# Two matmuls of 256 columns made into one of 512 in three of the seven products of a Strassen-like pair

## The chip, the cores and the metric

The kernel runs on one core of a Trainium2 chip. The metric is the device time of one execution in microseconds (us), as the median of several runs. Before the change it is 586.91 us (three runs, 586.62 to 586.93).

## The reference, cut to what matters

A mixture of eight experts with two tasks, for a batch of 512 rows:

```python
h = relu(einsum('bi,eio->beo', x, eW1) + eb1)           # 1024 -> 1024, per expert
h = relu(einsum('beh,eho->beo', h, eW2) + eb2)          # 1024 -> 512
expert_out = einsum('beh,eho->beo', h, eW3) + eb3       # 512 -> 256
gates = softmax(einsum('bi,tie->bte', x, gW) + gb, axis=-1)
tin = einsum('bte,bed->btd', gates, expert_out)
th = relu(einsum('btd,tdh->bth', tin, tW1) + tb1)       # 256 -> 512
th = relu(einsum('bth,tho->bto', th, tW2) + tb2)        # 512 -> 256
out = sigmoid(einsum('bth,tho->bto', th, tW3) + tb3)[..., 0]
```

All of it is float32.

## The kernel before

**Precision.** TensorE multiplies in the format fp32r. Each operand is split into a high part (the value rounded to fp32r) and a low part (the rest). One product is then three matmuls into one PSUM bank: high weights by high data, high weights by low data, low weights by high data (`triple`, L263 to L266). ScalarE makes the high parts (names ending in `_hi`), VectorE the low ones by a subtraction (names ending in `_lo`).

**Stages.** Layer 1 of expert 0 is done plainly, in 512-column matmuls, then layer 2 of expert 0. A loop follows with e from 1 to 7. In it TensorE does layer 1 of expert e as four *pairs*, then layer 3 of the expert before (24 matmuls of 512 columns), then layer 2 of expert e (96 matmuls of 512 columns). Behind the loop stand the last layer 3 and the two towers.

**A pair.** Layer 1 of experts 1 to 7 uses the seven products of a Strassen-Winograd scheme instead of eight. The 1024 outputs, the 1024 inputs and the batch are each cut in two; a pair i makes the output blocks i and 4 + i of 128 rows for both halves of the batch (256 columns each). `PRODUCTS` (L53) lists for each of the seven: the bank and the half of it that it writes, whether it reads x or `t` (differences of blocks of x, formed once), and which block. Each product has four contraction blocks of three matmuls with 256 columns, thus 84 matmuls a pair. A pair uses the banks 0 to 3 or, when i is odd, 4 to 7. In their order the products are called P2, P1, P4, P7, P5, P6, P3.

**Preparing a pair.** VectorE forms four sums of weight blocks (`sum31`, `sum2`, `sum4`; L763, L769, L775), ScalarE casts the three plain blocks and the four sums (`plain_hi`, `sums31_hi`, `sums24_hi`; L571, L577, L585 to L589), and VectorE makes the low parts (`plain_lo`, `sums31_lo`, `sums24_lo`, all through `split_lo`, L727). The weights lie in a ring of ten slots.

**Combining a pair.** ScalarE takes P1 out of its bank (`p1_take`, L597 and L598). VectorE adds the products up into `quarter`: `combine_base` (L808: P2 and P6 plus or minus P1), `combine_united` (L813: plus P7 and P5), `combine_lower` (L819), `combine_cross` (L825 and L828: P3 and P4). Its last operation raises the semaphore `combined`. ScalarE then writes the ReLU's high part (`pair_h1`, L602) and VectorE the low one (`pair_h1_lo`, through L738).

**What sets the order.** Each engine runs its own list, written by hand, and semaphores tie the lists. VectorE's list in the loop has three iterations (i = 0 to 2) that prepare pair i + 1 and, from i = 1, combine pair i - 1. Behind them stand a tail that combines pair 2, the splits of W3 and of three pieces of W2 (`w3_lo`, `w2_lo`), a tail that combines pair 3, the last piece of W2 and the gating of the expert before (`gate_expert`). TensorE waits for `slot_ready` (weights split) at the first, fourth and sixth product of a pair; for `combined` of pair i - 2 at the first product of pair i; and for `combined` of pair 3 at the start of layer 2, whose four banks (`BANK_HIDDEN2`) pair 3 has used. SP issues the weight loads, each held by a wait for `slot_ready`.

```python
                for i in range(PAIRS - 1):
                    if i > 0:
                        combine_base(e, i - 1)
                    sum31(e, i + 1)
                    if i > 0:
                        combine_united(e, i - 1)
                    sum2(e, i + 1)
                    if i > 0:
                        combine_lower(e, i - 1)
                        combine_cross(e, i - 1)
                    sum4(e, i + 1)
                    plain_lo(e, i + 1)
```

Of the kernel before, what the change touches and what calls it, by code (L numbers as in the profile page):

```python
# [13 lines left out]
P = 128  # L14
# [11 lines left out]
MG = 4  # L26
# [26 lines left out]
PRODUCTS = [(1, 0, "x", 1, 0),  # L53
            (0, 0, "x", 0, 0),
            (3, 0, "t", 1, 0),
            (2, 1, "t", 0, 1),
            (2, 0, "t", 0, 0),
            (1, 1, "t", 1, 1),
            (3, 1, "x", 1, 1)]
# [14 lines left out]
BANK_HIDDEN1 = [0, 1, 2, 3, 4, 5, 6, 7]  # L74
BANK_HIDDEN2 = [4, 5, 6, 7]
BANK_OUT3 = [0, 1]
BANK_LOGITS, BANK_GATES = 0, 1
BANK_TOWER1 = [[2, 3, 4, 5], [6, 7, 0, 1]]
BANK_TOWER2 = [[2, 3], [4, 5]]
BANK_FINAL = [6, 7]  # L80
# [35 lines left out]
def moe_towers(nc, xT, eW1_first, eW1_pairs, eW2, eW3, tW1, tW2, small, out):  # L116
    with ExitStack() as ctx:
# [6 lines left out]
        x_hi, x_lo = sb("x_hi", [KX, BATCH], F32R), sb("x_lo", [KX, BATCH], F32R)  # L124
        t_hi, t_lo = sb("t_hi", [KX, BATCH], F32R), sb("t_lo", [KX, BATCH], F32R)
        h1_hi, h1_lo = sb("h1_hi", [K2, BATCH], F32R), sb("h1_lo", [K2, BATCH], F32R)
# [13 lines left out]
        banks = [ctx.enter_context(nc.psum_tensor(f"bank{b}", [P, BATCH], F32)) for b in range(8)]  # L140
# [35 lines left out]
        def pair_of(h, i):  # L176
            return h[:].rearrange("p (g i) b -> p g i b", g=2)[:, :, i, :]
# [23 lines left out]
        lowered = sem("lowered")  # L201
        combined = sem("combined")
# [128 lines left out]
        def _(pe):  # L331
# [33 lines left out]
            def pair(e, i):  # L365
                ready = splits(e) + 3 * i
                for n, (bank, nh, source, kh, xh) in enumerate(PRODUCTS):
                    if n == 0:
                        if i == 0:

                            pe.wait_ge(gated_ready, 1 + GATED * (e - 1))
                        elif i == 1:
                            pe.wait_ge(h2_staged, K3 * e)
                        else:
                            pe.wait_ge(combined, PAIRS * (e - 1) + i - 1)
                        pe.wait_ge(slot_ready, ready + 1)
                    if n == 3:
                        pe.wait_ge(slot_ready, ready + 2)
                    if n == 5:
                        pe.wait_ge(slot_ready, ready + 3)  # L380
                    slot = (NP * i + n) % RING
                    to = banks[4 * (i % 2) + bank][:, nh * HALF:(nh + 1) * HALF]
                    hi, lo = (x_hi, x_lo) if source == "x" else (t_hi, t_lo)
                    for kk in range(KK):
                        cols = slice(kk * P, (kk + 1) * P)
                        mm = triple(pe, to, w_hi[:, slot, cols], w_lo[:, slot, cols],
                                    block_of(hi, kh, xh)[:, kk, :], block_of(lo, kh, xh)[:, kk, :],
                                    kk == 0, kk == KK - 1)
                    mm.then_inc(slot_used, 1)

            def layer2(e, between=None):
                first = isinstance(e, int)
                order = by_tile(range(0, 6), MG) + by_bank(range(6, 8), MG)
                for i, (n, m) in enumerate(order):
                    k = ORDER2[n]
                    if m == 0:
                        if n % 2 == 0:
                            pe.wait_ge(slot_ready, (KX + n // 2 + 1) if first
                                       else splits(e) + 3 * PAIRS + 1 + n // 2 + 1)
                        if first:  # L400
# [9 lines left out]
                    mm = triple(pe, banks[BANK_HIDDEN2[m]][:], w_hi[:, n, cols], w_lo[:, n, cols],  # L410
                                h1_hi[:, k, :], h1_lo[:, k, :], n == 0, n == K2 - 1)
# [86 lines left out]
            for t in range(T):  # L498
                pe.wait_ge(slot_ready, ready + T + t + 1)
                for i, (k, m) in enumerate(by_bank(range(KT2), KT1)):  # L500
                    if i < KT2:
                        pe.wait_ge(tower1_ready, t * KT2 + k + 1)
                    if k == 0:
                        pe.wait_ge(tower1_staged, 2 * t + m + 1)
                    slot = 2 * T + 2 * t + k // 2
                    cols = slice((k % 2) * TH2 + m * P, (k % 2) * TH2 + (m + 1) * P)
                    mm = triple(pe, banks[BANK_TOWER2[t][m]][:], w_hi[:, slot, cols], w_lo[:, slot, cols],
                                h1_hi[:, t * KT2 + k, :], h1_lo[:, t * KT2 + k, :], k == 0, k == KT2 - 1)
                    if k == KT2 - 1:
                        mm.then_inc(tower2_done, 1)  # L510
# [9 lines left out]
        def _(act):  # L520
# [21 lines left out]
            def take_first(m):  # L542
                act.wait_ge(sums_done, m + 1)
                bank, bias = banks[BANK_HIDDEN1[m]], prm_of("b1", m)
                act.activation(h1_hi[:, m, :], bank[:], ACT.Relu, bias=bias).then_inc(h1_taken, 1)
# [45 lines left out]
            def p1_take(e, i):  # L591
# [4 lines left out]
                p = banks[4 * (i % 2)][:, 0:HALF]  # L596
# [3 lines left out]
            def pair_h1(e, i):  # L600
                act.wait_ge(combined, PAIRS * (e - 1) + i + 1)
                act.activation(pair_of(h1_hi, i), stage[:], ACT.Relu).then_inc(h1_taken, 1)  # L602
# [50 lines left out]
            with act.Fori(1, E) as e:  # L653
# [67 lines left out]
        def _(dve):  # L721
# [18 lines left out]
            def first_h1_lo(m):  # L740
                dve.wait_ge(h1_staged, m + 1)
                relu_lo(h1_lo[:, m, :], stage[:, m % 2, :], h1_hi[:, m, :]).then_inc(h1_ready, 1)
# [53 lines left out]
            def bank_of(i, b):  # L796
                return banks[4 * (i % 2) + b][:].rearrange("p (h b) -> p h b", h=2)

            def combine_base(e, i):
# [8 lines left out]
                dve.tensor_tensor(quarter[:, 0:5:4, :], bank_of(i, 1), p1[:], ALU.add).then_inc(based, 1)  # L808

            def combine_united(e, i):  # L810

                dve.wait_ge(based, PAIRS * (e - 1) + i + 1)
                dve.tensor_tensor(quarter[:, 1:3, :], bank_of(i, 2), quarter[:, 4:5, :].broadcast_to([P, 2, HALF]),  # L813
                                  ALU.add).then_inc(united, 1)

            def combine_lower(e, i):

                dve.wait_ge(united, PAIRS * (e - 1) + i + 1)
                dve.scalar_tensor_tensor(quarter[:, 3, :], bank_of(i, 2)[:, 0, :], prm_of("b1", e * K2 + MG + i),  # L819
                                         quarter[:, 2, :], ALU.add, ALU.add).then_inc(lowered, 1)  # L820

            def combine_cross(e, i):

                dve.wait_ge(slot_used, used(e, NP * i + 6))
                dve.scalar_tensor_tensor(quarter[:, 1, :], bank_of(i, 3)[:, 1, :], prm_of("b1", e * K2 + i),  # L825
                                         quarter[:, 1, :], ALU.add, ALU.subtract)
                dve.wait_ge(lowered, PAIRS * (e - 1) + i + 1)
                dve.scalar_tensor_tensor(quarter[:, 2, :], bank_of(i, 3)[:, 0, :], prm_of("b1", e * K2 + MG + i),  # L828
                                         quarter[:, 2, :], ALU.add, ALU.add).then_inc(combined, 1)

            def pair_h1_lo(e, i):
                dve.wait_ge(h1_taken, K2 + PAIRS * (e - 1) + i + 1)
                relu_lo(pair_of(h1_lo, i), stage[:], pair_of(h1_hi, i)).then_inc(h1_ready, 1)
# [107 lines left out]
            with dve.Fori(1, E) as e:  # L941
# [9 lines left out]
                for i in range(PAIRS - 1):  # L951
# [18 lines left out]
                combine_cross(e, PAIRS - 2)  # L970
                pair_h1_lo(e, PAIRS - 2)
# [6 lines left out]
                combine_cross(e, PAIRS - 1)  # L978
                pair_h1_lo(e, PAIRS - 1)
# [130 lines left out]
```

## Time and profile before

| | us |
|---|---|
| median of three runs | 586.91 (586.62 to 586.93) |
| the profiled execution, its own time | 586.58 |
| its span, from first to last instruction | 584.9 |
| TensorE matmul busy | 577.5 (99%) |
| TensorE weight load busy | 520.9 (89%) |
| VectorE busy | 436.1 (75%) |
| ScalarE busy | 263.9 (45%) |
| GpSimd busy | 44.2 (8%) |

The granted clock of TensorE is 1.00 of full speed over the span. Matmuls are pipelined: each is shown for 283 ns (256 columns) or 389 ns (512 columns), while the next one begins earlier. What a matmul costs in a full stream is therefore the distance from start to start, not its duration. On VectorE too an instruction that waits for nothing begins before the one ahead of it has ended.

### The profile page before, as it was taken

How to read it: one execution, taken by the hardware profiler on the slowest of the kernel's cores; microseconds unless marked ns; L12 is line 12 of the kernel's file. 1: busy time of each engine (PE TensorE's matmuls, PEld its weight loads, DVE VectorE, ACT ScalarE, POOL GpSimd, SP SyncE). 2: the span in 40 equal slices, each digit the busy share in tenths (PEclk: the TensorE clock that was granted, in tenths of full speed). 3: DMA queues.
4: the chain of work that ended last, by engine and by line, in shares of the span. 5: the costliest groups of instructions: out<-in, count | busy, mean ns of one | idle time of the engine just before them, and what ended most of it. 6: DMA issues, size and time to landing. Idle time of an engine off the chain costs nothing.

```text
span 584.9 us, 9687 instructions
## 1 busy us (share of the span) xinstructions
PE 577.5 (99%) x3637; PEld 520.9 (89%) x3637; DVE 436.1 (75%) x534; ACT 263.9 (45%) x334; POOL 44.2 (8%) x46
## 2 busy tenths in 40 slices
PE   8999999999999999999999999999999999999997
PEld 5888889988999899988999889998999889998775
DVE  7954199874997569874898649985698749975492
ACT  3545174515645174522653255341645146542552
POOL 0000010030000300021000300003000300004000
PEclk9999999999999999999999999999999999999999
DMA  8340333243141513234223422316032332353000
GB/s 305 138 143 10 135 112 145 74 168 119 72 143 36 198 53 143 72 117 170 72 73 106 179 72 83 132 36 251 4 140 101 143 114 72 119 165 111 1 1 0
DMA packets 23276, 63.27 MB, mean 108 GB/s; under 512 B 1617, under 2 KB 6865, under 8 KB 19682
## 3 DMA queue, kind: packets, MB, share of 16 engines
q1 hardware_dynamic: 21906, 58.64, 28.3%
q0 software_dynamic: 1216, 4.23, 2.1%
q10 hardware_dynamic: 144, 0.26, 0.2%
q8 instruction: 7, 0.11, 0.1%
q14 instruction: 3, 0.02, 0.0%
HBM read 63.08 MB, written 0.04 MB: 108 GB/s over the span
## 4 chain that ended last, share of the span: by engine, by line
PE 95%; DVE 2%; DMA 1%; ACT 1%; issue 1%; SPq 0%; DVEq 0%
PE bank L264 31%; PE bank L266 31%; PE bank L265 31%; DMA w_raw<-eW_first 1%; DVE w_lo L727 1%; PE bank L441 0%; PE bank L442 0%; DVE scratch L763 0%; ACT w_hi L687 0%; ACT w_hi L530 0%; PE bank L516 0%; SPq L284 0%; DVE scratch L1043 0%; DVE scratch L1003 0%; ACT h_hi L624 0%
## 5 line engine op out<-in xcount | busy, mean ns | idle before, releaser
L264 PE MATMUL bank<-h_hi,w_hi 128*128 128x512 f32 x336 | 131.1, 390 | 0.8 <-DVE h_lo L738 0.8
L265 PE MATMUL bank<-h_lo,w_hi 128*128 128x512 f32 x336 | 130.8, 389 | 0.0
L266 PE MATMUL bank<-h_hi,w_lo 128*128 128x512 f32 x336 | 130.7, 389 | 0.0
L727 DVE TENSOR_TENSOR w_lo<-w_raw,w_hi 128x1024 fp32r<-128x1024 f32 (+1 forms) x79 | 111.3, 1420 | 25.5 <-ACT w_hi L540 8.1
L264 PE MATMUL bank<-x_hi,w_hi 128*128 128x256 f32 (+1 forms) x412 | 125.2, 304 | 1.8 <-DVE w_lo L727 1.1
L264 PE MATMUL bank<-t_hi,w_hi 128*128 128x256 f32 x448 | 126.8, 283 | 0.0
L265 PE MATMUL bank<-t_lo,w_hi 128*128 128x256 f32 x448 | 126.8, 283 | 0.0
L266 PE MATMUL bank<-t_hi,w_lo 128*128 128x256 f32 x448 | 126.8, 283 | 0.0
L265 PE MATMUL bank<-x_lo,w_hi 128*128 128x256 f32 (+1 forms) x412 | 124.7, 303 | 0.0
L266 PE MATMUL bank<-x_hi,w_lo 128*128 128x256 f32 (+1 forms) x412 | 124.7, 303 | 0.0
L738 DVE SCALAR_TENSOR_TENSOR h_lo<-scratch,h_hi 128x512 fp32r<-128x512 f32 (+1 forms) x68 | 61.8, 912 | 55.0 <-ACT scratch L625 34.9
L264 PEld LDWEIGHTS bank<-t_hi,w_hi 128*128 128x128 f32 x448 | 86.0, 192 | 0.0
L265 PEld LDWEIGHTS bank<-t_lo,w_hi 128*128 128x128 f32 x448 | 86.0, 192 | 0.0
L266 PEld LDWEIGHTS bank<-t_hi,w_lo 128*128 128x128 f32 x448 | 86.0, 192 | 0.0
L264 PEld LDWEIGHTS bank<-x_hi,w_hi 128*128 128x128 f32 x412 | 78.7, 191 | 6.6 <-DVE w_lo L727 2.1
L571 ACT ACTIVATE w_hi<-w_raw 128x1536 fp32r<-128x1536 f32 x28 | 41.8, 1492 | 93.8 <-PE bank L266 93.8
L265 PEld LDWEIGHTS bank<-x_lo,w_hi 128*128 128x128 f32 x412 | 78.7, 191 | 3.1
L266 PEld LDWEIGHTS bank<-x_hi,w_lo 128*128 128x128 f32 x412 | 78.7, 191 | 3.0
L264 PEld LDWEIGHTS bank<-h_hi,w_hi 128*128 128x128 f32 x336 | 63.1, 188 | 14.1 <-DVE h_lo L738 1.2
L266 PEld LDWEIGHTS bank<-h_hi,w_lo 128*128 128x128 f32 x336 | 63.1, 188 | 13.2
L265 PEld LDWEIGHTS bank<-h_lo,w_hi 128*128 128x128 f32 x336 | 63.1, 188 | 12.8
L727 DVE TENSOR_TENSOR w_lo<-scratch,w_hi 128x1024 fp32r<-128x1024 f32 x49 | 58.8, 1226 | 20.8 <-ACT w_hi L577 19.0
(95 smaller groups left out, 540.2 us busy)
## 6 DMA issues: line engine op xcount, KB each, us to landing
w_raw<-eW_pairs SPq DMA_DIRECT2D x28, 1024.0 KB, 4.8
w_raw<-eW SPq DMA_DIRECT2D x40, 512.0 KB, 3.7
scratch<-gates_dram POOLq DMA_DIRECT2D x8, 512.0 KB, 3.8
w_raw<-eW_first SPq DMA_DIRECT2D x7, 512.0 KB, 6.2
w_raw<-tW SPq DMA_DIRECT2D x4, 512.0 KB, 4.2
scratch<-xT SPq DMA_DIRECT2D x7, 256.0 KB, 6.4
w_raw<-eW_first SPq DMA_DIRECT2D x2, 256.0 KB, 4.2
scratch<-xT ACTq DMA_DIRECT2D x1, 256.0 KB, 3.4
```

What stands on the lines that cost most here:

```text
L264: pe.matmul(bank, weights_hi, moving_hi, start=first, stop=False)
L265: pe.matmul(bank, weights_hi, moving_lo, start=False, stop=False)
L266: return pe.matmul(bank, weights_lo, moving_hi, start=False, stop=last)
L571: act.activation(wide(pair_slots(i, 0, 3)), w_raw[:, u * UNIT:u * UNIT + 3 * SLOT], ACT.Copy) \
L727: dve.tensor_tensor(wide(w_lo, slots), raw, wide(w_hi, slots).bitcast(F32), ALU.subtract).then_inc(slot_ready, 1)
L738: return dve.scalar_tensor_tensor(lo, staged, 0.0, hi.bitcast(F32), ALU.max, ALU.subtract)
```

## The change

1. `PRODUCTS` now has for each product two places among the 16 half banks (for even and for odd i) and a flag. Where the flag is set (P2, P4 and P3) the matmul of the high weights reads the high and the low part of the x block at once, as two strips of 256 columns, and writes a whole bank: high by high into its first half, high by low into its second. The matmul of the low weights still has 256 columns and adds to the first half. The other four products stay as they were.
2. x and t hold their high and low parts in one tile each (`x_both`, `t_both`). The eight banks are one tensor. `h1_hi` and `h1_lo` are laid out by batch halves, so that layer 2 and the second tower layer read their 512 columns as two strips of 256.
3. The banks are given out anew. An even pair has 0, 1 and 2 for itself, an odd one 5, 6 and 7; bank 3 (P7 and P5) and bank 4 (P3) are shared by all pairs. Banks of layer 2: 5, 6, 7, 4.
4. TensorE gets new waits: at the fourth product for `lowered` of the pair before, at the sixth for `p1_staged` of its own pair, at the seventh for `combined` of the pair before (in pair 0 for `h2_staged`).
5. VectorE gets `combine_low`: two more adds a pair, which add the second halves of the three banks (512 and 256 elements). They now raise `combined`. `combine_lower` moves up behind `combine_united`. `combine_cross` waits for `lowered` ahead of both its operations.
6. ScalarE does `p1_take` before `pair_h1`, `sums31_hi` and `sums24_hi` instead of between the last two, and `p1_take` of pair 3 before `pair_h1` of pair 2 and the split of W3.

```diff
-PRODUCTS = [(1, 0, "x", 1, 0),
...
+PRODUCTS = [((0, 10), True, "x", 1, 0),
+            ((4, 14), False, "x", 0, 0),
+            ((2, 12), True, "t", 1, 0),
+            ((6, 6), False, "t", 0, 1),
+            ((7, 7), False, "t", 0, 0),
+            ((5, 15), False, "t", 1, 1),
+            ((8, 8), True, "x", 1, 1)]
+P2, P1, P4, P7, P5, P6, P3 = [places for places, *_ in PRODUCTS]
...
-BANK_HIDDEN2 = [4, 5, 6, 7]
+BANK_HIDDEN2 = [5, 6, 7, 4]
...
+        x_both, t_both = sb("x_both", [2, KX, BATCH], F32R), sb("t_both", [2, KX, BATCH], F32R)
+        h1_hi, h1_lo = sb("h1_hi", [2, K2, HALF], F32R), sb("h1_lo", [2, K2, HALF], F32R)
...
                     if n == 3:
+                        if i > 0:
+
+                            pe.wait_ge(lowered, PAIRS * (e - 1) + i)
                         pe.wait_ge(slot_ready, ready + 2)
                     if n == 5:
+
+                        pe.wait_ge(p1_staged, PAIRS * (e - 1) + i + 1)
                         pe.wait_ge(slot_ready, ready + 3)
+                    if n == 6:
+
+                        if i == 0:
+                            pe.wait_ge(h2_staged, K3 * e)
+                        else:
+                            pe.wait_ge(combined, PAIRS * (e - 1) + i)
...
+                        moving = both[:, :, kh * KK + kk, xh * HALF:(xh + 1) * HALF]
+                        if broad:
+                            two = halves_of_psum[:, places[i % 2]:places[i % 2] + 2, :]
+                            pe.matmul(two, w_hi[:, slot, cols], moving, start=(kk == 0), stop=False)
+                            mm = pe.matmul(to, w_lo[:, slot, cols], moving[:, 0, :], start=False, stop=(kk == KK - 1))
+                        else:
+                            mm = triple(pe, to, w_hi[:, slot, cols], w_lo[:, slot, cols],
+                                        moving[:, 0, :], moving[:, 1, :], kk == 0, kk == KK - 1)
...
                     plain_hi(e, i + 1)
+                    p1_take(e, i)
                     if i > 0:
                         pair_h1(e, i - 1)
                     sums31_hi(e, i + 1)
-                    p1_take(e, i)
                     sums24_hi(e, i + 1)
+                p1_take(e, PAIRS - 1)
                 pair_h1(e, PAIRS - 2)
                 w3_split(e)
-                p1_take(e, PAIRS - 1)
...
+            def combine_low(e, i):
+
+                dve.wait_ge(crossed, 2 * PAIRS * (e - 1) + 2 * i + 1)
+                dve.tensor_tensor(quarter[:, 0:2, :], several(P2[i % 2] + 1, P4[i % 2] + 1), quarter[:, 0:2, :], ALU.add)
+                dve.wait_ge(crossed, 2 * PAIRS * (e - 1) + 2 * i + 2)
+                dve.tensor_tensor(quarter[:, 2, :], halves_of_psum[:, P3[i % 2] + 1, :], quarter[:, 2, :],
+                                  ALU.add).then_inc(combined, 1)
...
                     if i > 0:
                         combine_united(e, i - 1)
+                    if i > 0:
+                        combine_lower(e, i - 1)
                     sum2(e, i + 1)
                     if i > 0:
-                        combine_lower(e, i - 1)
                         combine_cross(e, i - 1)
+                    if i > 0:
+                        combine_low(e, i - 1)
                     sum4(e, i + 1)
```

What the change moves, in the order of the instructions. First VectorE in the iteration i = 1 of the pair loop, from `combine_base` of pair 0 to the split of the plain blocks of pair 2 (`scratch` holds the sums and `quarter`, `prm` the biases). Before:

```order
L808 TENSOR_TENSOR scratch<-bank,scratch 128x2x256 [waits h2_ready]
L763 TENSOR_TENSOR scratch<-w_raw 128x1024 [waits slot_ready,landed0]
L813 TENSOR_TENSOR scratch<-bank,scratch 128x512 [waits based]
L769 TENSOR_TENSOR scratch<-scratch,w_raw 128x512 [waits summed]
L819 ISA [waits united]
L819 SCALAR_TENSOR_TENSOR scratch<-bank,prm,scratch 128x256
L825 ISA [waits slot_used]
L825 SCALAR_TENSOR_TENSOR scratch<-bank,prm,scratch 128x256
L828 SCALAR_TENSOR_TENSOR scratch<-bank,prm,scratch 128x256 [waits lowered]
L775 TENSOR_TENSOR scratch<-scratch,w_raw 128x512 [waits summed]
L727 TENSOR_TENSOR w_lo<-w_raw,w_hi 128x1536 [waits slot_hi]
```

The same place with the change:

```order
L837 TENSOR_TENSOR scratch<-psum,scratch 128x2x256 [waits h2_ready]
L790 TENSOR_TENSOR scratch<-w_raw 128x1024 [waits slot_ready,landed0]
L842 TENSOR_TENSOR scratch<-psum,scratch 128x512 [waits based]
L848 ISA [waits united]
L848 SCALAR_TENSOR_TENSOR scratch<-psum,prm,scratch 128x256
L796 TENSOR_TENSOR scratch<-scratch,w_raw 128x512 [waits summed]
L855 SCALAR_TENSOR_TENSOR scratch<-psum,prm,scratch 128x256 [waits lowered,slot_used]
L858 SCALAR_TENSOR_TENSOR scratch<-psum,prm,scratch 128x256
L865 TENSOR_TENSOR scratch<-psum,scratch 128x512 [waits crossed]
L867 TENSOR_TENSOR scratch<-psum,scratch 128x256 [waits crossed]
L802 TENSOR_TENSOR scratch<-scratch,w_raw 128x512 [waits summed]
L754 TENSOR_TENSOR w_lo<-w_raw,w_hi 128x1536 [waits slot_hi]
```

`combine_lower` (L819, now L848) stands directly behind `combine_united` (L813, now L842), and two adds (L865, L867) have come in ahead of `sum4` (now L802).

Second, TensorE where pair 1 ends (its last product, P3) and pair 2 begins (P2). Before, the last contraction block of P3 and the first of P2:

```order
L264 MATMUL bank<-x_hi,w_hi 128x256
L265 MATMUL bank<-x_lo,w_hi 128x256
L266 MATMUL bank<-x_hi,w_lo 128x256
L376 REGISTER_ALU [waits combined]
L264 MATMUL bank<-x_hi,w_hi 128x256 [waits slot_ready]
L265 MATMUL bank<-x_lo,w_hi 128x256
L266 MATMUL bank<-x_hi,w_lo 128x256
```

With the change, from the last matmul of P6 on through all of P3:

```order
L277 MATMUL psum<-t_both,w_lo 128x256
L411 MATMUL psum<-x_both,w_hi 128x512 [waits combined]
L412 MATMUL psum<-x_both,w_lo 128x256
L411 MATMUL psum<-x_both,w_hi 128x512
L412 MATMUL psum<-x_both,w_lo 128x256
L411 MATMUL psum<-x_both,w_hi 128x512
L412 MATMUL psum<-x_both,w_lo 128x256
L411 MATMUL psum<-x_both,w_hi 128x512
L412 MATMUL psum<-x_both,w_lo 128x256
L387 REGISTER_ALU [waits combined]
L411 MATMUL psum<-x_both,w_hi 128x512 [waits slot_ready]
```

A contraction block of these products is two matmuls where it was three, and P3 itself now waits for `combined`.

Third, ScalarE behind the cast of the plain blocks in the iteration i = 1. Before, `pair_h1` (L602) follows it, and with the change `p1_take` (L624, L625) does:

```order
L571 ACTIVATE w_hi<-w_raw 128x1536 [waits slot_used]
L602 ACTIVATE h_hi<-scratch 128x2x512 [waits combined]
L575 REGISTER_ALU
L561 REGISTER_ALU [waits summed]
L577 ACTIVATE w_hi<-scratch 128x1024 [waits slot_used]
```

```order
L598 ACTIVATE w_hi<-w_raw 128x1536 [waits slot_used]
L620 REGISTER_ALU
L624 ACTIVATE scratch<-psum 128x256 [waits based,slot_used]
L625 ISA
L625 ACTIVATE scratch<-psum,prm 128x256
```

The reading of P1 has moved ahead of the wait for `combined`.

## Rows read from the trace of the kernel before

**Rows 1.** The page: busy time by engine, and the chain by engine.

```profile
PE 577.5 (99%) x3637; PEld 520.9 (89%) x3637; DVE 436.1 (75%) x534; ACT 263.9 (45%) x334; POOL 44.2 (8%) x46
...
PE 95%; DVE 2%; DMA 1%; ACT 1%; issue 1%; SPq 0%; DVEq 0%
```

**Rows 2.** Stretches: us, then PE, PEld, DVE, ACT, POOL busy (instructions), PEclk, DMA share, GB/s.

```profile
212.44:222.51 10.07, 10.07 (x86) 10.07 (x84) 9.51 (x10) 6.41 (x9) 0.00 (x0) 1.00 0.12 41
222.51:232.59 10.08, 10.08 (x87) 10.08 (x85) 10.08 (x15) 5.17 (x7) 0.00 (x0) 1.00 0.44 163
...
252.75:279.98 27.23, 27.23 (x123) 22.53 (x121) 14.94 (x18) 8.16 (x10) 5.55 (x5) 1.00 0.35 135
...
117.67:144.90 27.23, 27.23 (x123) 22.53 (x121) 16.48 (x20) 8.17 (x10) 5.57 (x5) 1.00 0.40 148
```

**Rows 3.** Timeline at a restart of TensorE (start, duration in us, line, operation).

```profile
75.25 1.75 DVE L727 TENSOR_TENSOR w_lo<-w_raw,w_hi 128x1536 fp32r<-128x1536 f32 x1
...
77.06 0.39 PE L264 MATMUL bank<-x_hi,w_hi 128*128 128x256 f32 x1 [0.41 <-DVE w_lo L727]
77.28 0.28 PE L265 MATMUL bank<-x_lo,w_hi 128*128 128x256 f32 x1
```

**Rows 4.** Timeline of VectorE, iteration i = 1 of an ordinary expert.

```profile
221.91 0.69 DVE L808 TENSOR_TENSOR scratch<-bank,scratch 128x512 f32<-128x512 f32 x1
222.51 1.22 DVE L763 TENSOR_TENSOR scratch<-w_raw 128x1024 f32<-128x1024 f32 x1
223.65 0.69 DVE L813 TENSOR_TENSOR scratch<-bank,scratch 128x512 f32<-128x512 f32 x1
224.25 0.69 DVE L769 TENSOR_TENSOR scratch<-scratch,w_raw 128x512 f32<-128x512 f32 x1
224.85 0.48 DVE L819 SCALAR_TENSOR_TENSOR scratch<-bank,prm,scratch 128x256 f32<-128x256 f32 x1
225.24 0.48 DVE L825 SCALAR_TENSOR_TENSOR scratch<-bank,prm,scratch 128x256 f32<-128x256 f32 x1
...
231.76 0.70 DVE L808 TENSOR_TENSOR scratch<-bank,scratch 128x512 f32<-128x512 f32 x1
```

**Rows 5.** Timeline of VectorE, tails of pairs 2 and 3 in that expert.

```profile
241.55 0.70 DVE L808 TENSOR_TENSOR scratch<-bank,scratch 128x512 f32<-128x512 f32 x1
242.28 0.69 DVE L813 TENSOR_TENSOR scratch<-bank,scratch 128x512 f32<-128x512 f32 x1
243.12 0.48 DVE L819 SCALAR_TENSOR_TENSOR scratch<-bank,prm,scratch 128x256 f32<-128x256 f32 x1
...
245.51 1.23 DVE L738 SCALAR_TENSOR_TENSOR h_lo<-scratch,h_hi 128x1024 fp32r<-128x1024 f32 x1 [1.12 <-ACT h_hi L602]
246.65 1.22 DVE L727 TENSOR_TENSOR w_lo<-w_raw,w_hi 128x1024 fp32r<-128x1024 f32 x1
248.04 2.36 DVE L727 TENSOR_TENSOR w_lo<-w_raw,w_hi 128x1024 fp32r<-128x1024 f32 x2 [0.17 <-ACT w_hi L614]
251.16 1.23 DVE L727 TENSOR_TENSOR w_lo<-w_raw,w_hi 128x1024 fp32r<-128x1024 f32 x1 [0.76 <-ACT w_hi L614]
252.30 0.69 DVE L808 TENSOR_TENSOR scratch<-bank,scratch 128x512 f32<-128x512 f32 x1
...
254.65 0.48 DVE L828 SCALAR_TENSOR_TENSOR scratch<-bank,prm,scratch 128x256 f32<-128x256 f32 x1
```

**Rows 6.** Timeline of ScalarE: the third piece of W2.

```profile
250.07 1.06 ACT L614 ACTIVATE w_hi<-w_raw 128x1024 fp32r<-128x1024 f32 x1 [1.12 <-PE bank L266]
```

**Rows 7.** Timeline of VectorE in the first trip of the loop.

```profile
89.47 0.69 DVE L808 TENSOR_TENSOR scratch<-bank,scratch 128x512 f32<-128x512 f32 x1
...
115.59 3.50 DVE L727 TENSOR_TENSOR w_lo<-w_raw,w_hi 128x1024 fp32r<-128x1024 f32 x3 [0.17 <-ACT w_hi L614]
...
121.35 0.47 DVE L828 SCALAR_TENSOR_TENSOR scratch<-bank,prm,scratch 128x256 f32<-128x256 f32 x1
```

**Rows 8.** Timeline of VectorE during layer 2, with its idle time ahead in brackets.

```profile
210.05 0.69 DVE L738 SCALAR_TENSOR_TENSOR h_lo<-scratch,h_hi 128x512 fp32r<-128x512 f32 x1 [3.26 <-ACT scratch L625]
```

More of the change, by code:

```diff
@@ L139, in moe_towers @@
         squash_sink = sb("squash_sink", [1])
-        banks = [ctx.enter_context(nc.psum_tensor(f"bank{b}", [P, BATCH], F32)) for b in range(8)]
+        psum = ctx.enter_context(nc.psum_tensor("psum", [P, 8 * BATCH], F32))
+        banks = [psum[:, b * BATCH:(b + 1) * BATCH] for b in range(8)]
+        halves_of_psum = psum[:].rearrange("p (h b) -> p h b", h=16)
         gates_dram = nc.dram_tensor("gates_dram", [E, T, BATCH], F32, kind="Internal").ap()
@@ L366, in pair @@
                 ready = splits(e) + 3 * i
-                for n, (bank, nh, source, kh, xh) in enumerate(PRODUCTS):
+                for n, (places, broad, source, kh, xh) in enumerate(PRODUCTS):
                     if n == 0:
@@ L506, in _ @@
                     cols = slice((k % 2) * TH2 + m * P, (k % 2) * TH2 + (m + 1) * P)
-                    mm = triple(pe, banks[BANK_TOWER2[t][m]][:], w_hi[:, slot, cols], w_lo[:, slot, cols],
-                                h1_hi[:, t * KT2 + k, :], h1_lo[:, t * KT2 + k, :], k == 0, k == KT2 - 1)
+                    mm = triple(pe, halved(banks[BANK_TOWER2[t][m]]), w_hi[:, slot, cols], w_lo[:, slot, cols],
+                                h1_hi[:, :, t * KT2 + k, :], h1_lo[:, :, t * KT2 + k, :], k == 0, k == KT2 - 1)
                     if k == KT2 - 1:
@@ L595, in p1_take @@
                     act.wait_ge(based, PAIRS * (e - 1) + i)
-                p = banks[4 * (i % 2)][:, 0:HALF]
+                p = halves_of_psum[:, P1[i % 2], :]
                 act.activation(p1[:, 1, :], p, ACT.Copy, scale=-1.0)
@@ L601, in pair_h1 @@
                 act.wait_ge(combined, PAIRS * (e - 1) + i + 1)
[L602 removed]
+                act.activation(pair_of(h1_hi, i), quarter[:, 0:4, :], ACT.Relu).then_inc(h1_taken, 1)
             def w3_split(e):
@@ L794, in sums24_lo, with several @@
                                       ALU.subtract).then_inc(slot_ready, 1)
-            def bank_of(i, b):
-                return banks[4 * (i % 2) + b][:].rearrange("p (h b) -> p h b", h=2)
+            def several(*places):
+                step = places[1] - places[0]
+                return halves_of_psum[:, places[0]:places[-1] + 1:step, :]
             def combine_base(e, i):
@@ L807, in combine_base @@
                     dve.wait_ge(h1_ready, K2 + PAIRS * (e - 1) + i)
-                dve.tensor_tensor(quarter[:, 0:5:4, :], bank_of(i, 1), p1[:], ALU.add).then_inc(based, 1)
+                dve.tensor_tensor(quarter[:, 0:5:4, :], several(P2[i % 2], P6[i % 2]), p1[:], ALU.add).then_inc(based, 1)
             def combine_united(e, i):
                 dve.wait_ge(based, PAIRS * (e - 1) + i + 1)
-                dve.tensor_tensor(quarter[:, 1:3, :], bank_of(i, 2), quarter[:, 4:5, :].broadcast_to([P, 2, HALF]),
-                                  ALU.add).then_inc(united, 1)
+                dve.tensor_tensor(quarter[:, 1:3, :], several(P7[i % 2], P5[i % 2]),
+                                  quarter[:, 4:5, :].broadcast_to([P, 2, HALF]), ALU.add).then_inc(united, 1)
@@ L816, in combine_lower @@
             def combine_lower(e, i):
                 dve.wait_ge(united, PAIRS * (e - 1) + i + 1)
-                dve.scalar_tensor_tensor(quarter[:, 3, :], bank_of(i, 2)[:, 0, :], prm_of("b1", e * K2 + MG + i),
-                                         quarter[:, 2, :], ALU.add, ALU.add).then_inc(lowered, 1)
+                dve.scalar_tensor_tensor(quarter[:, 3, :], halves_of_psum[:, P5[i % 2], :],
+                                         prm_of("b1", e * K2 + MG + i), quarter[:, 1, :], ALU.add, ALU.add).then_inc(lowered, 1)
@@ L970, in _ @@
                 combine_cross(e, PAIRS - 2)
+                combine_low(e, PAIRS - 2)
                 pair_h1_lo(e, PAIRS - 2)
@@ L978, in _ @@
                 combine_cross(e, PAIRS - 1)
+                combine_low(e, PAIRS - 1)
                 pair_h1_lo(e, PAIRS - 1)
```

55 lines of the change are left out of this document (25 added, 30 removed).

## Prediction

> **What bounds the kernel now.** I read the page first. TensorE is busy 99% of the span and carries 95% of the chain that ended last [rows 1], so any time comes out of its stream of matmuls or out of new gaps in it. I then read its busy time by stage in one ordinary expert (e = 3, the third trip of the loop) [rows 2]. A pair is 7 products of 4 contraction blocks of 3 matmuls, that is 84 matmuls of 256 columns, in 10.08 us: 120.0 ns each. Layers 3 and 2 are 24 + 96 = 120 matmuls of 512 columns in 27.23 us: 226.9 ns each. The reader should see two things. TensorE has no gap in either stretch. And 512 columns cost 13.1 ns less than twice 256, since 2 x 120.0 is 240.0; that is all the change can win. An expert is 4 x 10.08 + 27.23 = 67.55 us.
>
> VectorE is busy 75% on average, which hides where it is full: in the window of that pair it is busy 10.08 of 10.08 us. Its instructions from one `combine_base` to the next stand back to back, 9.85 us apart (221.91 to 231.76) [rows 4]. So in the pairs VectorE has 2% to spare. It lives on a lead, and gets its idle time back in layer 2.
>
> **TensorE's part of the change.** Three of seven products put two matmuls of 256 into one of 512: 3 x 4 = 12 merged couples a pair, 48 an expert, 336 in all over 7 experts. At 13.1 ns a pair takes 9.92 us, an expert's pairs 0.63 us less, the kernel 4.4 us less. A merged matmul reads two strips of x 16 KB apart, and layer 2 and the second tower layer now read their 512 columns as two strips too; no row shows that form. The nearest rows are the plain 512 at 226.9 ns (no cost, taken, since each strip is a run of 256 and the bank is written in one run) and two separate 256 (13.1 ns more).
> The Trainium skill ("TensorE: Matmul & The Clock Gate", section "Wait — 56ns, not 53.3ns?") gives a warm matmul's start-to-start time as columns over 2.4 GHz plus about 2.5 ns. By that a merge would save 0.8 us in the kernel, not 4.4. The rows differ: both 120.0 and 226.9 ns stand about 13 ns above columns over 2.4 GHz, at a granted clock of 1.00, so the measurement decides. By the page's figure rival 1 below would end at 586.1, and the forecast would not move: TensorE would reach layer 2 at 258.1, still ahead of VectorE.
>
> The warm-up, the first expert and the towers keep their matmul counts. The new waits of TensorE on semaphores already counted cost nothing by themselves: pairs start today with two waits and no gap [rows 2].
>
> **VectorE's part.** `combine_low` adds per pair one add of 512 and one of 256 elements. Steps from start to start, unhindered: 1.14 us for 1024 elements, 0.60 for 512 (222.51 to 223.65 to 224.25), 0.39 for a 256-element operation with a scalar (224.85 to 225.24) [rows 4]. On the line through the first two, 256 elements take 0.33; bounds 0.33 and 0.42 (its full duration, by the line through the durations 1.22 and 0.69 of the same rows). Taken: 0.60 + 0.33 = 0.93 us; with full durations 0.69 + 0.42 = 1.11.
> `combine_lower` moves up to stand right behind `combine_united`, whose result it waits for. In the tails, where no sums stand between, this adjacency exists already: 242.28 to 243.12, 0.84 us where 0.60 is the free step [rows 5]. So +0.24 in each of the two loop iterations (bound below: 0), and with the adds 0.93 + 0.24 = **1.17 us** an iteration.
> The tails of pairs 2 and 3 take 2.83 us today (241.55 to the end of the last operation, as 252.30 to 254.65 + 0.48) [rows 5]. Now: base 0.73 and united 0.84 as there, lower 0.52 (its 0.48 and a hop of 0.04, as the 0.73 is 0.69 and a hop, because the first cross operation now waits for it), cross 0.39 twice, the 512 add 0.60, and 0.42 to the end of the 256 add: 3.89, **+1.06 us** each. When the last pair is combined, VectorE is later by 2 x 1.17 + 2 x 1.06 = 4.46 us.
>
> What absorbs it: behind pair 2 VectorE waits for ScalarE's splits of W2, shown as 0.17 and 0.76. By start-to-start steps it is more: 246.65 to 248.04 is 0.25 over the free 1.14, and the third split at 251.16 is 0.85 behind 248.04 + 2 x 1.14, together 1.10 us [rows 5]. The second is ScalarE waiting for TensorE to free a slot at 250.07 [rows 6], which it will have done. The 1.12 us wait for `pair_h1` of pair 2 stays, being a dependency. So `combined` of pair 3 comes 4.46 - 1.10 = 3.36 us later, at 254.65 + 0.48 + 3.36 = **258.49**. Layer 2 waits for it (banks 5, 6, 7, 4). TensorE started layer 2 at 252.75 + 24 x 0.2269 = 258.20 with 3.07 us of slack; now it is there at 257.57. It stands 0.92 us, then restarts: 0.05 from release to start, and 0.10 for the first matmul, as at 77.06 (0.22 to the next start where 0.12 is the step, behind a VectorE end at 77.00) [rows 3]. Layer 2 starts at 258.64, **0.44 us later** than before.
>
> Earlier deadlines in that expert hold, if narrowly. I shift the rows by the sums above: `lowered` of pair 1 is there at 235.99, needed at 236.5; `lowered` of pair 2 at 245.94, needed at 246.4; the plain split of pair 3 at 240.6, needed at 242.2; W3's split at 251.3, needed at 252.1. The take of P1 on ScalarE, moved ahead of `pair_h1` and now awaited by the sixth product, needs only the second product and `based`, over 3 us ahead. `pair_h1` is behind it 0.8 us at most and VectorE reaches its low part later still. SP's next loads wait for splits that move by these amounts and land over 3 us before use. After a late layer 2 the lateness dies: VectorE idles 3.26 us at one place in layer 2 alone, about as much as it is late, [rows 8], and its next start is tied to the end of that layer 2. So the loss is once an expert, six times: 6 x 0.44 = +2.6 us.
>
> **The first trip of the loop** is worse, for its VectorE begins later: `combine_base` of pair 0 stands 12.41 us behind the pair's first matmul (77.06, 89.47) against 9.47 (212.44, 221.91) [rows 2 to 4], and its three W2 splits run together with 0.17 idle [rows 7]. Absorbed: 0.25, not 1.10. `combined` comes at 121.35 + 0.47 + 4.21 = 126.03, TensorE restarts effectively at 126.2, and layer 2 there started at 117.67 + 5.45 = 123.12 [rows 2]: **+3.1 us**. TensorE will also stand about 0.9 us at the fourth product of pairs 1 and 2, for `lowered`; that lies within the 3.1.
>
> **Sum**: 2.6 + 3.1 = +5.7 us. The 4.4 us are spent in it, since VectorE's chain sets the time of every expert. On the profiled execution's 586.58 this is 592.3; the median 586.91 is 0.33 above that execution, so the forecast is **592.6**. About 0.2% (1.2 us) is what a measurement of this kernel can tell from no change.
>
> **Rivals.**
> 1. TensorE stays the bound: faster. It needs VectorE's growth under (3.07 - 0.63 + 1.10) / 4 = 0.88 us a pair; the two adds alone, with every stall hidden, are 0.93, just above. For it: dependencies cost nothing inside the iterations today [rows 4]. Against: the adds' steps are known, and the tails have nothing to hide a dependency behind. In full it gives 586.91 - 4.4 = 582.5; Between it and the forecast the ordinary experts gain 0.3 and the first loses some 2: 585 to 588.
> 2. The two-strip form costs. 96 x 8 of layer 2 and 48 of the towers, at the 13.1 ns of a separate matmul, are 816 x 13.1 = 10.7 us, and VectorE's chain starts at layer 2's end, so it adds in full: 603. Against: nothing in the rows asks for it.
> 3. Stalls add up: every new VectorE step runs at its full duration and the cross operations stall like `combine_lower` (+0.15). Growth 1.11 + 0.24 + 0.15 = 1.5 us a pair, or 6.0 an expert; layer 2 starts 6.0 - 4.46 = 1.5 us later still, 7 x 1.5 = +10.8: 603.
> That the merge does not happen is excluded by the order of instructions shown with the change: the 512-column matmuls and both adds stand there.
>
> **Chances.** Forecast (588.1 to 597) 0.72; rival 1 in full 0.08, half-way within 0.2% 0.07 and below that 0.02; rivals 2 and 3, or a mild form of them above 597, 0.11. So faster 0.10, same 0.07, slower 0.83. The range leaves out rival 1 in full and the far ends of 2 and 3: from 587.5 (pure step sum: 4 x 0.93 = 3.72, ordinary experts -0.3, first +2.3) to 599.
>
> **What would show it.** Right: TensorE idle about 0.9 to 1.1 us before layer 2 in experts 2 to 7 of the loop, released by the last add of `combine_low`; 512-column matmuls of x and t at 227 ns; iterations of VectorE at 11.0 us; two stalls near 0.9 us in the first trip. Wrong: no such idle (rival 1), layer 2 longer than 96 x 0.227 us (rival 2), idle of 2 us or more (rival 3).

## The result and the profile after

The changed kernel takes 594.12 us (median of four runs, 593.82 to 594.33), against 586.92 us (586.62 to 587.62) for the kernel before on the same chip. The ratio is 1.0125, with a 95% interval of 1.0113 to 1.0137: slower by 7.2 us. The forecast was 592.6 us, with a range of 587.5 to 599. The profiled execution took 594.08 us, its span is 592.4.

The page of the changed kernel, busy time by engine and then the chain by engine:

```profile
PE 577.4 (97%) x3301; PEld 502.2 (85%) x3301; DVE 464.1 (78%) x590; ACT 265.1 (45%) x334; POOL 44.2 (7%) x46
...
PE 38%; DVE 36%; issue 19%; ACT 4%; DVEq 1%; DMA 1%; SPq 0%; ACTq 0%
```

Against [rows 1] TensorE has 336 matmuls fewer and the same busy time, and it is no longer alone on the chain: VectorE holds 36% of it. VectorE has 56 instructions and 28.0 us more, which is 28 pairs times 1.00 us of shown time.

TensorE's own waits, in total, with count and the longest:

```profile
PE psum L275 <- DVE scratch L867: 5.7, 7, 1.3
PE psum L275 <- DVE scratch L848: 1.6, 2, 0.8
```

These two are new. L867 is the last add of `combine_low`: seven waits, one a trip, at the start of layer 2. L848 is `combine_lower`: two waits, both in the first trip. The same ordinary expert as in [rows 2], in two stretches (the four pairs, then layers 3 and 2), with us, then busy time of PE, PEld, DVE, ACT and POOL:

```profile
216.69:256.62 39.93, 39.93 (x289) 37.74 (x288) 37.63 (x48) 22.05 (x29) 0.00 (x0) 1.00 0.22 79
256.62:284.90 28.28, 27.55 (x122) 22.45 (x121) 18.63 (x23) 8.54 (x11) 5.58 (x5) 1.00 0.42 148
```

The pairs are down from 40.31 to 39.93 us, without a gap. Layers 3 and 2 are up from 27.23 to 28.28, and TensorE is idle in 0.73 of it. The expert takes 68.21 us instead of 67.54, in each of the last six trips (68.18 to 68.22).

VectorE in the iteration that answers to [rows 4]:

```profile
226.17 0.68 DVE L837 TENSOR_TENSOR scratch<-psum,scratch 128x512 f32<-128x512 f32 x1
226.77 1.21 DVE L790 TENSOR_TENSOR scratch<-w_raw 128x1024 f32<-128x1024 f32 x1
227.90 0.68 DVE L842 TENSOR_TENSOR scratch<-psum,scratch 128x512 f32<-128x512 f32 x1
228.76 0.48 DVE L848 SCALAR_TENSOR_TENSOR scratch<-psum,prm,scratch 128x256 f32<-128x256 f32 x1 [0.18 <-DVE scratch L842]
229.16 0.68 DVE L796 TENSOR_TENSOR scratch<-scratch,w_raw 128x512 f32<-128x512 f32 x1
...
230.55 0.68 DVE L865 TENSOR_TENSOR scratch<-psum,scratch 128x512 f32<-128x512 f32 x1
231.14 0.41 DVE L867 TENSOR_TENSOR scratch<-psum,scratch 128x256 f32<-128x256 f32 x1
231.47 0.68 DVE L802 TENSOR_TENSOR scratch<-scratch,w_raw 128x512 f32<-128x512 f32 x1
...
237.22 0.68 DVE L837 TENSOR_TENSOR scratch<-psum,scratch 128x512 f32<-128x512 f32 x1
```

The iteration takes 11.05 us (226.17 to 237.22) instead of 9.85. The two adds step by 0.59 and 0.33. `combine_lower` starts 0.86 behind `combine_united`, where the free step is 0.60; the profile even shows the 0.18 in which VectorE waits for itself.

The tail of pair 3, as the second half of [rows 5], and the start of layer 2:

```profile
258.93 0.68 DVE L837 TENSOR_TENSOR scratch<-psum,scratch 128x512 f32<-128x512 f32 x1
259.64 0.69 DVE L842 TENSOR_TENSOR scratch<-psum,scratch 128x512 f32<-128x512 f32 x1
260.48 0.48 DVE L848 SCALAR_TENSOR_TENSOR scratch<-psum,prm,scratch 128x256 f32<-128x256 f32 x1
261.07 0.48 DVE L855 SCALAR_TENSOR_TENSOR scratch<-psum,prm,scratch 128x256 f32<-128x256 f32 x1
261.47 0.48 DVE L858 SCALAR_TENSOR_TENSOR scratch<-psum,prm,scratch 128x256 f32<-128x256 f32 x1
261.86 0.68 DVE L865 TENSOR_TENSOR scratch<-psum,scratch 128x512 f32<-128x512 f32 x1
262.46 0.41 DVE L867 TENSOR_TENSOR scratch<-psum,scratch 128x256 f32<-128x256 f32 x1
...
261.90 0.39 PE L277 MATMUL psum<-h_hi,w_lo 128*128 128x512 f32 x1
263.02 0.47 PE L275 MATMUL psum<-h_hi,w_hi 128*128 128x512 f32 x1 [0.73 <-DVE scratch L867]
```

The last matmul of layer 3 starts at 261.90, so TensorE was due at 261.90 + 0.23 = 262.13 and starts at 263.02, 0.89 later. By the span the account is: 6 x 0.67 = 4.0 us in the last six trips; 3.31 in the first (from its first matmul to its layer 2: 77.24 to 126.63, against 77.06 to 123.14); 0.18 ahead of the loop, where the kernels of this case differ by more than that without a cause in their lists (the loop's first matmul stands at 76.8 us in the run without the adds and at 77.4 in the one with the old order). Together 7.5 us, as 592.4 - 584.9.

### The profile page after: what moved, and what is told of

It reads as the page before. It is cut to its first block, busy times and chain, and to the rows that moved or that the text cites. A ratio compares the mean times of both kernels' runs of the same rounds, so it can differ in the third digit from the quotient of the medians.

```text
span 592.4 us, 9183 instructions
## 1 busy us (share of the span) xinstructions
PE 577.4 (97%) x3301; PEld 502.2 (85%) x3301; DVE 464.1 (78%) x590; ACT 265.1 (45%) x334; POOL 44.2 (7%) x46
## 4 chain that ended last, share of the span: by engine, by line
PE 38%; DVE 36%; issue 19%; ACT 4%; DVEq 1%; DMA 1%; SPq 0%; ACTq 0%
PE psum L275 13%; DVE w_lo L754 13%; PE psum L276 12%; PE psum L277 12%; DVE scratch L790 5%; DVE scratch L842 3%; DVE h_lo L765 3%; DVE scratch L867 2%; DVE scratch L837 2%; DVE scratch L855 2%; DVE scratch L802 1%; DVE scratch L848 1%; DVE scratch L796 1%; ACT h_hi L629 1%; ACT w_hi L612 1%
## 5 line engine op out<-in xcount | busy, mean ns | idle before, releaser
L275 PE MATMUL psum<-h_hi,w_hi 128*128 128x512 f32 x336 | 131.9, 393 | 6.5 <-DVE scratch L867 5.7
L277 PE MATMUL psum<-h_hi,w_lo 128*128 128x512 f32 x336 | 130.9, 390 | 0.0
L276 PE MATMUL psum<-h_lo,w_hi 128*128 128x512 f32 x336 | 130.8, 389 | 0.0
L275 PE MATMUL psum<-t_both,w_hi 128*128 128x256 f32 x336 | 95.4, 284 | 1.6 <-DVE scratch L848 1.6
L277 PE MATMUL psum<-t_both,w_lo 128*128 128x256 f32 x336 | 95.3, 284 | 0.0
L276 PE MATMUL psum<-t_both,w_hi 128*128 128x256 f32 x336 | 95.1, 283 | 0.0
L275 PEld LDWEIGHTS psum<-h_hi,w_hi 128*128 128x128 f32 x336 | 63.1, 188 | 22.7 <-issue 8.5
L411 PE MATMUL psum<-x_both,w_hi 128*128 128x512 f32 x224 | 80.5, 398 | 0.4 <-DVE w_lo L754 0.4
L275 PEld LDWEIGHTS psum<-t_both,w_hi 128*128 128x128 f32 x336 | 63.4, 189 | 3.5 <-issue 2.4
L277 PEld LDWEIGHTS psum<-t_both,w_lo 128*128 128x128 f32 x336 | 63.5, 189 | 0.0
L276 PEld LDWEIGHTS psum<-t_both,w_hi 128*128 128x128 f32 x336 | 63.5, 189 | 0.0
L275 PE MATMUL psum<-x_both,w_hi 128*128 128x256 f32 (+1 forms) x188 | 61.5, 327 | 1.5 <-DVE w_lo L754 0.8
L412 PE MATMUL psum<-x_both,w_lo 128*128 128x256 f32 x224 | 62.8, 281 | 0.0
L276 PE MATMUL psum<-x_both,w_hi 128*128 128x256 f32 (+1 forms) x188 | 61.3, 326 | 0.0
```

The costliest lines, as they stand in the source:

```text
L275: pe.matmul(bank, weights_hi, moving_hi, start=first, stop=False)
L276: pe.matmul(bank, weights_hi, moving_lo, start=False, stop=False)
L277: return pe.matmul(bank, weights_lo, moving_hi, start=False, stop=last)
L411: pe.matmul(two, w_hi[:, slot, cols], moving, start=(kk == 0), stop=False)
L412: mm = pe.matmul(to, w_lo[:, slot, cols], moving[:, 0, :], start=False, stop=(kk == KK - 1))
```

## The experiments

The theory: VectorE's chain from the end of layer 2 to `combined` of pair 3 sets when the next layer 2 starts, and the merged matmuls save time that nobody waits for. The rivals: TensorE itself pays (for the merged form, the shared banks or the new waits), or a wait that is taken away only moves on. Every run is compared with the kernel before on the same chip, 586.6 us (19 runs, 586.25 to 587.17 in the first two groups), 586.68 for the last two runs.

### The adds away

```diff
-                    if i > 0:
-                        combine_low(e, i - 1)
...
-                                         ALU.add, ALU.subtract).then_inc(crossed, 1)
+                                         ALU.add, ALU.subtract).then_inc(combined, 1)
```

> The changed kernel without combine_low: the second halves of the three banks (high weights by low data) are written by TensorE and never added, combined is raised by the last cross operation. TensorE's list is untouched. Theory (VectorE's chain up to combined of pair 3 sets the start of layer 2): the chain is about 1 us shorter per pair, so TensorE reaches layer 2 after combined; the ordinary expert falls from 68.21 us to 4 x 9.985 + 27.23 = 67.17, the first trip keeps one stall at lowered (pair 1, 0.8 us) and loses the one of pair 2; 585.6 us, a little under the kernel before. Rival (the merged matmuls, the shared banks or the new waits cost TensorE the time): 593 to 594, as TensorE's list is the same.

Measured: 585.60 us (585.18 to 585.99), ratio 0.9983 (0.9974 to 0.9993). This kernel leaves out a part of the products and serves the timing alone. In each ordinary expert the pairs take 39.93 us and layers 3 and 2 take 27.26, no wait at layer 2; the one stall at `lowered` is left, as expected. With TensorE's list untouched the 8.5 us are gone. That rules out the rival that TensorE pays: the seven waits for L867 were VectorE's chain.

### The merge undone, everything else kept

```diff
-                            pe.matmul(two, w_hi[:, slot, cols], moving, start=(kk == 0), stop=False)
...
+                        for kk in range(KK):
+                            pe.matmul(to_low, w_of(w_hi, kk), moving(kk)[:, 1, :], start=(kk == 0), stop=(kk == KK - 1))
```

> The changed kernel with each merged matmul taken apart again: four high-by-low matmuls of 256 columns into the second half bank, then the high-by-high and low-by-high ones into the first. The same banks, waits and VectorE work. Pairs on TensorE go from 9.985 back to 10.08 us. Theory: TensorE arrives at layer 2 about 0.38 us later an expert, still ahead of combined (it waits 0.8 us there), so the time stays: 594.1, at most +0.3 from the first trip. Rival 1 (TensorE's stream is the bound): 336 x 8 ns = +2.7, 596.8. Rival 2 (the 512-column form on two strips is what costs): down towards 587 to 590.

Measured: 593.94 us (593.64 to 594.12), ratio 1.0126, the changed kernel's own. The ordinary expert again, and TensorE's wait for the last add (L874 in this kernel):

```profile
216.23:256.54 40.31, 40.31 (x337) 40.30 (x336) 38.01 (x49) 22.40 (x29) 0.00 (x0) 1.00 0.22 79
256.54:284.45 27.91, 27.51 (x122) 22.46 (x121) 18.27 (x22) 8.17 (x11) 5.56 (x5) 1.00 0.39 149
...
PE psum L275 <- DVE scratch L874: 3.6, 7, 1.2
```

The pairs are 0.38 us longer, the rest 0.37 shorter, the sum 68.22 against 68.21. What TensorE wins by merging it waits away: in the changed kernel the merge is worth nothing, and it costs nothing.

### Two splits of W2 moved behind the combination of pair 3

```diff
-                for i in range(3):
-                    w2_lo(e, i)
+                w2_lo(e, 0)
                 combine_base(e, PAIRS - 1)
...
                 combine_low(e, PAIRS - 1)
+                w2_lo(e, 1)
                 pair_h1_lo(e, PAIRS - 1)
+                w2_lo(e, 2)
```

> The changed kernel with VectorE's list reordered at one place: the splits of the second and third piece of W2 move from ahead of the combination of pair 3 to behind it (the second directly behind it, the third behind pair_h1_lo). Theory: combined of pair 3 comes 2 x 1.14 = 2.27 us earlier, TensorE no longer waits at layer 2; ordinary expert 67.17 us (-1.04, six times), first trip -1.5 us because TensorE is there at 125.1 where it started at 126.6: 594.1 - 7.7 = 586.4 us. Rival: the wait only moves on, to slot_ready or h1_ready within layer 2 or to the gates of the expert before: 590 to 594.

Measured: 586.40 us (586.06 to 586.85), ratio 0.9997 (0.9987 to 1.0006): the whole loss is back, by moving two instructions, with the same work. The stretches of an ordinary expert, and of TensorE's waits the one for VectorE's combination that is left:

```profile
213.69:253.62 39.93, 39.93 (x290) 37.74 (x289) 37.63 (x48) 22.02 (x29) 0.00 (x0) 1.00 0.23 79
253.62:280.88 27.26, 27.26 (x123) 22.53 (x121) 18.56 (x23) 8.55 (x11) 5.55 (x5) 1.00 0.43 154
...
PE psum L275 <- DVE scratch L848: 1.6, 2, 0.8
```

TensorE is idle nowhere in the expert. The two splits are needed 5.4 and 10.9 us into layer 2, and the wait did not move on to them.

### The dependent operations in their old order, the adds kept

```diff
+                    sum2(e, i + 1)
                     if i > 0:
                         combine_lower(e, i - 1)
-                    sum2(e, i + 1)
```

In `combine_cross` the operation on P3, which needs no `lowered`, comes first again, and the add of 256 goes ahead of the one of 512.

> The changed kernel (adds of combine_low and all) with the order of the dependent operations as before: sum2 stands between combine_united and combine_lower, and of the cross operations the one that needs no lowered comes first, so no operation of VectorE stands right behind the one that it waits for in the iterations; the 256 add goes ahead of the 512 add. Theory (the two adds are 0.93 of the growth, the rest is dependency stalls): VectorE's chain is 0.24 us shorter an iteration and 0.19 a tail, 0.86 an expert, and combined of pair 3 then ties with TensorE's arrival at layer 2 (45.32 against 45.38 us from the start of pair 0): period 67.2 us in six trips, -0.86 in the first, 587.2 us. Rival (the adds alone fill VectorE, order is nothing): 593 to 594.

Measured: 587.57 us (587.41 to 587.98), ratio 1.0017 (1.0007 to 1.0026). The iteration on VectorE that held the 0.86 step:

```profile
236.96 0.68 DVE L842 TENSOR_TENSOR scratch<-psum,scratch 128x512 f32<-128x512 f32 x1
237.56 0.69 DVE L796 TENSOR_TENSOR scratch<-scratch,w_raw 128x512 f32<-128x512 f32 x1
238.16 0.48 DVE L848 SCALAR_TENSOR_TENSOR scratch<-psum,prm,scratch 128x256 f32<-128x256 f32 x1
238.56 0.47 DVE L854 SCALAR_TENSOR_TENSOR scratch<-psum,prm,scratch 128x256 f32<-128x256 f32 x1
```

All steps are free ones. The ordinary expert takes 67.31 us, 0.12 over what TensorE alone needs, so the tie was nearly met. Of the 7.2 us lost, 6.5 hang on where dependent operations stand, although the adds are the bulk of VectorE's extra time. The run moves three things at once (`sum2`, the cross operations, the two adds); what each is worth alone was not measured. It is a threshold: the adds used up the slack, and the stalls came on top. In the first trip the old order has a price: `lowered` comes later there and TensorE's longest wait for it grows from 0.8 to 1.1 us.

### The first trip: gates turned earlier

```diff
-                    if between is not None and i in (len(order) // 4, 3 * len(order) // 4):
+                    if between is not None and i in (len(order) // 4, 14):
```

This moves TensorE's transposes of the gates inside layer 2 of expert 0. It was tried on the kernel with the late W2 splits and on the kernel before.

> The kernel of e3_w2_late with TensorE's four transposes of the gates moved from three quarters of expert 0's layer 2 to item 14 of 32, some 7 us earlier. VectorE waits 9.6 us for them ahead of the loop; now it starts the first trip's sums about 7 us earlier. Theory (the first trip is dear only because VectorE starts late there): the two stalls at lowered (1.0 and 0.93 us in start-to-start steps), the wait at pair 0 (0.57) and at pair 1 (about 0.1) go: 586.4 - 2.6 = 583.8 us. Rival: something else holds the first trip (the landing of the first pair's weights, or ring slots still in use by layer 2 of expert 0), and the stalls stay: 586.

> The kernel before the change with the early gates alone, to see what of e4 has nothing to do with the change. Theory: only the wait at pair 0 (0.57 us) and at pair 1 (0.1) go, as VectorE's lateness costs nothing later there: 585.9 us. Rival (early gates help any of these kernels alike): 584.

Measured: 583.45 us (583.21 to 583.66), ratio 0.9947 (0.9930 to 0.9963), and for the kernel before 585.73 us (585.56 to 586.19), ratio 0.9986 (0.9976 to 0.9996). No wait at L848 or L411 is left in the first. The same edit gives 2.95 us to the changed kernel with the late splits (586.40 to 583.45) and 0.9 to the one before: the first trip was dear because VectorE began it late, and only with the change was there no slack to carry that.

### The matmuls of a merged product grouped

The four of 512 columns first, then the four of 256:

```diff
-                    for kk in range(KK):
+                    for low_part in ((False, True) if broad else (None,)):
+                        for kk in range(KK):
```

> The kernel of e3_w2_late with the eight matmuls of a merged product in another order: the four of 512 columns first, then the four of 256. TensorE is the bound in this kernel, so a pair's length counts. In the changed kernel a merged matmul takes 232 ns, not 226.9. If the alternation of 512 and 256 columns costs the 5 ns: pairs of 9.92 us, 28 x 0.065 = -1.8, 584.6 us. If the read of two strips 16 KB apart costs them: no change, 586.4.

> The kernel of e5_w2_grouped with the high and the low strip of a merged matmul 2 KB apart (block by block in one tile) instead of 16 KB. Grouping brought the merged matmul from 232 to about 230 ns, 3 above the plain 512. If the distance of the strips costs those 3 ns: pairs 39.82 to 39.68 us an expert, 584.5. If they come from each change between 512 and 256 columns, or from having two strips at all: no change, 585.5 us.

Measured: 585.50 us (585.21 to 585.78) grouped, 585.82 us (585.61 to 586.21) with near strips. The pairs of an ordinary expert, grouped and then grouped with near strips:

```profile
213.63:253.45 39.82, 39.82 (x290) 37.72 (x288) 37.51 (x48) 21.93 (x29) 0.00 (x0) 1.00 0.22 79
```

```profile
214.07:253.88 39.81, 39.81 (x289) 37.72 (x288) 37.51 (x48) 21.91 (x29) 0.00 (x0) 1.00 0.22 79
```

Grouping takes 0.11 us from an expert, 2.3 ns a merged matmul, less than half of the 5 I looked for. Over seven trips that is 0.8 us, as measured (0.9). The distance of the strips does nothing. The pairs still miss 39.68 by 0.14 us an expert, and the grouped kernel's rows show where it comes from. The first merged product of the expert comes behind layer 2, so behind matmuls of 512 columns; another one comes behind twelve matmuls of 256 columns:

```profile
213.63 1.07 PE L417 MATMUL psum<-x_both,w_hi 128*128 128x512 f32 x4
214.54 0.64 PE L414 MATMUL psum<-x_both,w_lo 128*128 128x256 f32 x4
...
226.41 1.09 PE L417 MATMUL psum<-t_both,w_hi 128*128 128x512 f32 x4
227.34 0.63 PE L414 MATMUL psum<-t_both,w_lo 128*128 128x256 f32 x4
```

Four matmuls of 512 columns take 0.91 us in the first case, 227 ns each, and 0.93 in the second, about 232 each. Both read two strips, so the strips cost nothing. What costs is to come behind matmuls of 256 columns, and grouping takes away only some of those places.

### All three together

> W2 splits late, gates early and the merged products grouped, all three. Theory: the gains add, 586.4 - 2.6 - 1.8 = 582.0 us if the alternation costs, 583.8 if only the gates help.

Measured: 582.41 us (582.10 to 582.79), ratio 0.9928 (0.9911 to 0.9944). This is the fastest kernel of the study, 4.2 us under the one before. The fair rival for the merge is the kernel before with the same early gates, 585.73: by that the merge with a repaired order is worth 3.3 us, or 0.6%. The first trip's pairs and layers in it (the first window begins 0.15 us early, in the last matmul of layer 2; the pairs' first matmul starts at 76.95):

```profile
76.80:116.76 39.96, 39.96 (x290) 37.83 (x289) 37.51 (x48) 22.06 (x29) 0.00 (x0) 1.00 0.23 80
116.76:144.01 27.25, 27.25 (x122) 22.53 (x121) 18.71 (x23) 8.68 (x11) 5.58 (x5) 1.00 0.42 154
```

Its pairs take 39.81 us and it is now an expert like the others, 67.06 us each.

## Why the prediction was right

**The mechanism and its place** were as forecast: VectorE's chain to `combined` of pair 3, one wait a trip at the start of layer 2, two stalls at `lowered` in the first trip. Taking away the adds, moving work out of the chain and removing its stalls each brought the time that the sums gave, within 0.4 us; undoing the merge moved nothing.

**The sum** was 1.5 us short (+5.7 against +7.2), well inside the range. Its terms, forecast and measured in an ordinary expert:

| term | forecast | measured |
|---|---|---|
| one iteration | +1.17 | +1.20 and +1.16 (11.05 against 9.85, 10.95 against 9.79) |
| one tail | +1.06 | +1.12 (248.17 to 252.12) and +1.11 |
| `combined` of pair 3, from the first matmul of pair 0 | 46.05 | 46.18 |
| from there to the first matmul of layer 2 | 0.05 | 0.15 |
| longer expert | +0.44 | +0.67 |

The tail was mis-sized at one hop: I gave the step from `combine_lower` to the first cross operation 0.52 us and it takes 0.59, twice an expert. The release of TensorE was read from the restart at 77.06 [rows 3] as 0.05; here it is 0.15. Together that is the 0.23 us missing, which over six experts makes 1.4 us.

**The first trip** was forecast at +3.1 and is +3.3. Its stalls at `lowered` are 0.8 us each as shown, and about 1.0 from start to start.

**TensorE's saving** was put at 13.1 ns a merged matmul from two uniform streams, and is 0.38 / 48 = 7.9 ns. The step that failed is the one that took the plain 512 at 226.9 ns for the merged one; among matmuls of 256 it costs 232. The kernel before already showed this surcharge, in the first matmuls of layer 3 behind a pair (last section); the mean over 120 matmuls hid it. Since TensorE waits for VectorE anyway, this did not touch the time (the run with the merge undone shows it), but it would have put rival 1 at 584.3 us instead of 582.5.

**The rivals.** Rival 1 needed a growth below 0.88 us a pair; it is 1.15. Rival 2: layer 2 on two strips takes 227.2 ns a matmul with its layer 3, so nothing. Rival 3 had dependency stalls at every cross operation and full durations. The steps of the two adds are 0.59 and 0.33, free ones, and in the iterations the cross operations step freely too (0.39, 229.76 to 230.15). In the tails its stall is real: the first cross operation comes 0.20 behind its free step, where the sum had 0.13. The narrow deadlines that I had checked (pairs 2 and 3 at `lowered`, W3's split) held: TensorE has no gap in 216.69 to 256.62.

## What to carry to other kernels

An engine at 75% on average can be the one without slack: lay out its instructions between two points where it meets the bottleneck engine, and count what stands ahead of the operation that is waited for. A saving on the bottleneck engine that is paid for on another is worth something only if that chain is shortened too; here the cure was to move work that is needed later behind the operation that is needed now. When operations depend on each other on one in-order engine, an independent one between them costs nothing and saves up to a quarter of a microsecond.

## What the runs showed of the hardware

A matmul of 512 columns among matmuls of 256 costs more than one in a stream of its kind: 232 ns against 227 as a mean, and about 230 when four stand together. I had expected the two rates to hold in a mixed stream. In `L411` and `L412` the pattern can be read from start to start, at a granted clock of 1.00:

```profile
149.17 0.40 PE L411 MATMUL psum<-x_both,w_hi 128*128 128x512 f32 x1
149.41 0.28 PE L412 MATMUL psum<-x_both,w_lo 128*128 128x256 f32 x1
149.53 0.40 PE L411 MATMUL psum<-x_both,w_hi 128*128 128x512 f32 x1
149.77 0.28 PE L412 MATMUL psum<-x_both,w_lo 128*128 128x256 f32 x1
```

The 512 takes 0.24, the 256 behind it 0.12.

The merged form has no part in it. In the kernel before, where every matmul reads one strip, layer 3 begins behind a pair like this:

```profile
252.75 0.40 PE L264 MATMUL bank<-h_hi,w_hi 128*128 128x512 f32 x1
...
253.91 0.39 PE L266 MATMUL bank<-h_hi,w_lo 128*128 128x512 f32 x1
```

The first five steps take 1.16 us, 232 ns each, and those after them 227. Why the first matmuls of 512 behind matmuls of 256 are slower, no run shows.

The hop of a dependent step on VectorE is not one number: 0.03 us behind an operation's end for `combine_united` (258.93 + 0.68 to 259.64), 0.15 for `combine_lower` (259.64 + 0.69 to 260.48), and 0.11 for the first cross operation (260.48 + 0.48 to 261.07). `combine_lower` has one more instruction between the wait and the operation, `L848 ISA` in the order of instructions; that this makes the difference was not tested.

An independent operation on VectorE starts before the one ahead is shown to end: 512 elements last 0.68 us and step by 0.59 (230.55 to 231.14), 256 last 0.41 and step by 0.33 (231.14 to 231.47). The Trainium skill ("VectorE: DVE Perf Modes", section "The DRAIN you can't avoid") says that the next operation does not start until the pipe is empty, but that one which is not held starts earlier. By the durations shown the trace agrees with the second half: the overlap is about 0.09 us. The same section of the Trainium skill says of eight copies in a row that a semaphore after each costs nothing extra. Here a wait for the operation just ahead takes the overlap away and adds the hop: 0.71 us from `combine_base` to `combine_united` and 0.84 from there to `combine_lower`, where 0.60 is the free step.
